# Cross attention with a mixture of experts on one core: the last batch whole in the second half, fewer warm transposes, logits read from PSUM, new orders

## The chip, the cores and the metric

The kernel runs on one core of a Trainium2 chip. The metric is the device time of one execution in microseconds (us), the median of several runs. TensorE (PE), VectorE (DVE), ScalarE (ACT), GpSimd (POOL) and SyncE (SP) each work off their own queue in order; they wait for each other on semaphores. VectorE, ScalarE and TensorE reach PSUM, eight banks of 512 fp32 columns; GpSimd works on SBUF alone.

## The reference

x is (4, 512, 128), the context is (4, 77, 96). Cut to what matters:

```python
xn = layernorm(ctx, ln_x_g, ln_x_b)                    # 77 x 96 a batch
ln = layernorm(_layernorm(x), ln_l_g, ln_l_b)          # 512 x 128 a batch
q  = ln @ Wq.T                                         # 2 heads of 64
k, v = split(concat([xn @ Wkv.T, ln @ Wlkv.T], axis=1))   # 77 + 512 keys
attn = softmax(where(mask, (rmsnorm(q)*SCALE) @ rmsnorm(k).T, -max))
x = x + (attn @ v) @ Wo.T + bo
l2 = _layernorm(x)
gates = softmax(l2 @ Wg + bg)                          # 8 experts
top2 = top_k(gates, 2)                                 # not renormalised
out = x + sum over top2 of gate * (l2 @ We[e] + be[e])
```

All is fp32. The masked context columns get the largest negative number before the softmax.

## The kernel before

Each batch is 4 tiles of 128 tokens. The first half of the work (normalise, q, k, v) is cut into the parts of FRONT, each (batch, first tile, end tile): batch 0 in two parts of two tiles, the others whole, so FRONT part 2 is batch 1, part 3 batch 2, part 4 batch 3. The second half (scores, exponentials, values, projection, second layernorm, gate, experts) is cut into the parts of REAR; before the change these are batches 0 to 2 whole and batch 3 as two parts, 3 and 4, of two tiles.

There is no scheduler at run time. Four texts, TENSOR, VECTOR, SCALAR and GPSIMD, list the jobs of each engine in the order of its queue: name, part, and a number within the part. TENSOR also names the PSUM banks that a job writes; `free` lets the job wait until the last user of each bank has been read. `walk` issues the jobs. The third number of `warm` is a slot; its second number says how many transposes of the identity that job issues, into a bank that nobody reads.

The jobs which the prediction speaks of:

- `warm` (L923), `weights` (L930, L932) and `weights2` (L940, L942): transposes of the identity, and of the weight matrices. ScalarE's `weights` and `weights2` (L498, L503, L504) copy the latter out of PSUM.
- `stats1`, `rstd1`, `apply1`, `xT`, `lnT`: first layernorm. `q`, `qsq` (square, ScalarE), `ssq` (sum, L733, VectorE), `rq` (the power -1/2, L396, GpSimd), `qn` (L742), `qT`, `QH` and `QL`: the query, split into a rounded fp32r part and the rest. `k`, `kL`, `ssk`, `msk`, `rk` (L402) are the same for keys. Scores are three matmuls each (high x high, high x low, low x high).
- `ctx_apply` (L789) and other `ctx_` jobs: the context's part of keys and values. `mask`, `maskT`, `cbias`: the mask as a bias.
- `score p n` (n = 0 to 3 for key tiles, 4 for the context), `exp p n` (L602, L605; two instructions, one a head), `value p n`. `e01`, `e23` (L421, L430, GpSimd) and `esum1`, `esum2` (L803, L810, VectorE) sum the exponentials over key tiles; `den`, `dens`, `denT` turn that sum.
- `xbo` (L442, GpSimd): x plus bias bo, into one of two buffers; from batch 2 on it waits for the `x2` of two batches earlier. `proj`, `x2` (L822, L826, L830): the first half's result. `stats2`, `rstd2` (L448 to L451), `apply2` (L629), `l2T`, `l2L`, `gate` (L1121).
- `shifted` (L378, GpSimd) and `split` (L714, L716, VectorE): expert weights less their last row, and split in two. The two DMAs of the bias row lie between them (SyncE waits for `shifted`).
- `logits` (L850 to L860), `gexp`, `top` (L868 to L873): the largest logit, the two largest, the weights w. `low` (ScalarE, L660) scales four experts' output from PSUM by w, `high` (VectorE, L892) multiplies the other four and adds them up: number n of `high` on VectorE covers two tiles, eight instructions. `pair` and `res` (L473, L474, L482, GpSimd) add the two halves, and SyncE stores (L349).

Of the kernel before, what the change touches and what calls it, by code (L numbers as in the profile page):

```python
# [1169 lines left out]
```

## Time and profile before

| | |
|---|---|
| runs | 121.44, 122.02, 121.33 us; median 121.44 |
| the profiled execution | 120.44 us |
| its span in the profile | 118.6 us |
| PE | 105.5 us busy, 89%, 733 matmuls |
| DVE | 79.4 us, 67%, 317 instructions |
| ACT | 85.9 us, 72%, 209 |
| POOL | 92.3 us, 78%, 113 |
| granted TensorE clock, mean | 0.97 |
| chain that ended last | POOL 38%, PE 27%, DVE 18%, issue 11%, ACT 3% |

The span runs from the first to the last event of the one profiled execution. A busy share is an average over stages with different limits. Ends of matmuls are modelled, so a busy PE is not one at its peak. "Idle before" in a row is the time in which the engine stood still just before the instruction, and the arrow names what released it.

### The profile page before, as it was taken

What the parts mean: (1) busy time and instruction counts of PE and PEld (TensorE: products, weight loads), DVE (VectorE), ACT (ScalarE), POOL (GpSimd) and SP (SyncE); (2) the same over time, 40 slices, a digit from 0 to 9 for tenths busy, and PEclk for the clock granted to TensorE, in tenths of its full rate; (3) what the DMA queues carried; (4) which work ended last, traced back from release to release, by engine and by line L of the source; (5) the groups of instructions that cost most, each with busy time, mean ns of one, the idle gap of its engine ahead of it and who ended that gap; (6) DMA issues with size and microseconds to landing.
All of it is one profiled execution on the core that took longest, in us unless ns stands there. A gap on an engine that the chain in (4) does not pass through costs nothing.

```text
span 118.6 us, 2507 instructions
## 1 busy us (share of the span) xinstructions
PE 105.5 (89%) x733; PEld 74.5 (63%) x733; DVE 79.4 (67%) x317; ACT 85.9 (72%) x209; POOL 92.3 (78%) x113
## 2 busy tenths in 40 slices
...
DMA packets 6679, 3.92 MB, mean 33 GB/s; under 512 B 2314, under 2 KB 6282, under 8 KB 6667
## 3 DMA queue, kind: packets, MB, share of 16 engines
...
## 4 chain that ended last, share of the span: by engine, by line
POOL 38%; PE 27%; DVE 18%; issue 11%; ACT 3%; POOLq 1%; DVEq 0%; ACTq 0%
PE PS L923 8%; DVE part L892 6%; PE PS L1068 6%; POOL esum L421 5%; PE PS L1047 5%; POOL rq L396 4%; POOL e L430 4%; POOL xbo L442 4%; POOL rk L402 3%; POOL rstd L388 3%; PE PS L1102 2%; DVE acc L892 2%; POOL pair L473 2%; POOL rstd L450 2%; POOL We L378 2%
## 5 line engine op out<-in xcount | busy, mean ns | idle before, releaser
L602 ACT ACTIVATE probs<-PS,shift,rk 128x512 f32<-128x512 f32 (+1 forms) x40 | 25.0, 694 | 4.6 <-PE PS L1047 4.4
L660 ACT ACTIVATE scaled<-PS,w 128x128 f32<-128x128 f32 x64 | 17.4, 385 | 4.6 <-PE PS L916 3.7
L1068 PE MATMUL PS<-probs,V_sb 128*64 128x512 f32 (+1 forms) x80 | 16.1, 519 | 0.0
L914 PE MATMUL PS<-WeH,l2H 128*128 128x512 f32 x32 | 13.5, 423 | 1.8 <-ACT scaled L660 0.9
L473 POOL TENSOR_TENSOR pair<-scaled 128x512 f32<-128x512 f32 x8 | 10.3, 1286 | 4.0 <-ACT scaled L660 3.6
L916 PE MATMUL PS<-WeH,l2L 128*128 128x512 f32 x32 | 12.6, 393 | 0.0
L915 PE MATMUL PS<-WeL,l2H 128*128 128x512 f32 x32 | 12.5, 391 | 0.0
L430 POOL TENSOR_TENSOR e<-probs,probs 128x1024 f32<-128x1024 f32 (+1 forms) x5 | 9.7, 1931 | 3.0 <-ACT probs L602 3.0
L421 POOL TENSOR_TENSOR esum<-probs,probs 128x1024 f32<-128x1024 f32 (+1 forms) x5 | 10.7, 2141 | 1.1 <-ACT probs L602 1.1
L923 PE MATMUL PS<-ident 128*128 128x128 f32 x60 | 9.4, 324 | 1.5 <-POOL ident L366 1.5
L1047 PE MATMUL PS<-QH,KH 64*128 64x512 f32 (+1 forms) x40 | 9.0, 435 | 1.3 <-DVE QL L773 0.7
L923 PEld LDWEIGHTS PS<-ident 128*128 128x128 f32 x60 | 8.8, 172 | 1.5 <-POOL ident L366 1.5
L629 ACT ACTIVATE l<-x,nm,rstd 128x127 f32<-128x127 f32 x16 | 6.7, 490 | 3.7 <-POOL nm L451 3.7
L402 POOL TENSOR_TENSOR rk<-msk,half 128x8 f32<-128x8 f32 (+1 forms) x5 | 7.9, 1582 | 1.5 <-DVE msk L750 1.5
L1068 PEld LDWEIGHTS PS<-probs,V_sb 128*64 128x64 f32 x80 | 4.9, 136 | 6.3 <-issue 5.1
L892 DVE SCALAR_TENSOR_TENSOR part<-PS,w,part 128x128 f32<-128x128 f32 x32 | 8.9, 336 | 0.0
L914 PEld LDWEIGHTS PS<-WeH,l2H 128*128 128x128 f32 x32 | 6.1, 191 | 4.1 <-ACT scaled L660 1.3
L803 DVE TENSOR_TENSOR esum<-esum,e 128x1024 f32<-128x1024 f32 (+1 forms) x5 | 5.5, 1107 | 4.7 <-POOL e L430 4.7
L733 DVE TENSOR_REDUCE ssq<-qsq 128x8 f32<-128x512 f32 (+1 forms) x5 | 2.9, 579 | 8.6 <-ACT qsq L535 8.6
L396 POOL TENSOR_TENSOR rq<-msq,half 128x8 f32<-128x8 f32 (+1 forms) x5 | 7.3, 1465 | 0.4
L1047 PEld LDWEIGHTS PS<-QH,KH 64*128 64x128 f32 x40 | 4.1, 189 | 5.6 <-issue 2.8
L1047 PE MATMUL PS<-QH,KL 64*128 64x512 f32 (+1 forms) x40 | 7.6, 361 | 0.0
...
## 6 DMA issues: line engine op xcount, KB each, us to landing
out_dram<-x SPq DMA_DIRECT2D x8, 128.0 KB, 1.7
...
x_sb<-in_x_dram SPq DMA_DIRECT2D x2, 128.0 KB, 2.5
Wlkv_sb<-in_L_xattn_Wlkv_dram ACTq DMA_DIRECT2D x1, 128.0 KB, 3.0
...
```

Source lines behind the costliest of these rows:

```text
L421: pool.tensor_tensor(esum[p % 2][:, :, s], probs[p % 2][0][:, :, s], probs[p % 2][1][:, :, s], ALU.add).then_inc(e01_made, 1)
L430: pool.tensor_tensor(e23[:, :, s], probs[p % 2][2][:, :, s], probs[p % 2][3][:, :, s], ALU.add).then_inc(e23_made, 1)
L473: step(pool.tensor_tensor(pair[:], scaled[m % 2][:, :, 0:EH // 2], scaled[m % 2][:, :, EH // 2:EH], ALU.add))
L602: act.activation(probs[p % 2][n][:, h, s], ps[:, s], ACT.Exp, bias=shift[:, 0:1], scale=rk[:, b, n, h:h + 1]).then_inc(probs_made, 1)
L660: last = act.activation(scaled[m // 2 % 2][:, m % 2, e], ps[:, e], ACT.Copy, scale=w[:, m, e:e + 1])
L892: last = dve.scalar_tensor_tensor(dst, bank("high", p, 2 * n + k)[:, e * C:(e + 1) * C], w[:, m, EH + e:EH + e + 1], src, ALU.mult, ALU.add)
L914: pe.matmul(dst, lH, rH, start=True, stop=False)
L915: pe.matmul(dst, lH, rL, start=False, stop=False)
L916: return pe.matmul(dst, lL, rH, start=False, stop=True)
L923: pe.transpose(bank("warm", p, n)[:, 0:P], ident[:], ident[:])
L1047: last = pe.matmul(bank("score", p, n, h)[0:P if n < T else M, 0:(e - a) * P], k, queries[r, b % 2, a * P:e * P], start=(step == 0), stop= ...
L1068: last = pe.matmul(bank("value", p, 0)[h * D:(h + 1) * D, s], v, pr, start=(n == 0), stop=(n == KT - 1))
```

## The change

REAR takes batch 3 as one part, so the second half has four parts instead of five; its score, exponential, esum, x2, logits and other instructions of that batch are over 512 columns or four tiles each. The warm transposes go from 35 + 3 + 11 + 11 = 60, all ahead of the first q, to 14 + 1 + 4 + 4 there, 1 after v 0 and 2 ahead of the first score. The four orders and the bank numbers are written anew; k 0 now comes ahead of v 0, proj 0 and x2 0 right behind the values of batch 0, and all jobs of batch 3's score stand before its gate. In `logits` the subtraction of the largest logit reads the logits from PSUM instead of the SBUF copy, the bank is released by it, and the copy of the two largest becomes a reduction over an axis of one element. `cbias` does its first step in place in PSUM.

```diff
--- before.py
+++ after.py
@@ -20,62 +20,57 @@
 
 
 FRONT = ((0, 0, 2), (0, 2, 4), (1, 0, 4), (2, 0, 4), (3, 0, 4))
-REAR = ((0, 0, 4), (1, 0, 4), (2, 0, 4), (3, 0, 2), (3, 2, 4))
+REAR = ((0, 0, 4), (1, 0, 4), (2, 0, 4), (3, 0, 4))
 
 
 
 TENSOR = """
-    warm 0 35 7   weights 0 0 0   warm 1 3 7   weights2 0 0 1   warm 2 11 7   xT 0 0 2   warm 3 11 7   q 0 0 3
-    v 0 0 4   xT 1 0 5   k 0 0 6   ctxT 0 0 7   v 1 0 0   q 1 0 1   ssk 0 0 2   ctx_v 0 0 4   qT 0 0 5   k 1 0 7
-    ctx_k 0 0 3   maskT 0 0 0   qT 1 0 4   ssk 1 0 1   ctx_ss 0 0 2   score 0 0 05   score 0 1 61   xT 2 0 4
-    score 0 2 72   score 0 3 05   k 2 0 4   q 2 0 3   v 2 0 1   value 0 0 6   value 0 1 -   value 0 2 -
...
-    high 1 1 0   high 1 2 2   l2T 3 0 7   low 1 1 6   gate 2 0 3   low 1 2 4   low 1 3 5   high 1 3 6
-    high 2 0 0   low 2 0 1   gate 3 0 4   l2T 4 0 3   low 2 1 7   low 2 2 5   gate 4 0 2   low 2 3 6   low 3 0 3
-    low 3 1 1   high 2 1 4   high 2 2 7   high 2 3 2   high 3 0 5   high 3 1 6   low 4 0 0   low 4 1 4
-    high 4 0 3   high 4 1 1
+    warm 0 14 7   weights 0 0 0   warm 1 1 7   weights2 0 0 1   warm 2 4 7   xT 0 0 2   warm 3 4 7   q 0 0 3
+    k 0 0 4   xT 1 0 5   v 0 0 6   warm 4 1 7   ssk 0 0 7   ctxT 0 0 0   q 1 0 1   k 1 0 2   ctx_v 0 0 6
+    qT 0 0 4   ssk 1 0 5   ctx_k 0 0 0   maskT 0 0 7   v 1 0 3   qT 1 0 6   ctx_ss 0 0 5   warm 5 2 1
+    score 0 0 14   score 0 1 32   score 0 2 06   xT 2 0 5   score 0 3 14   value 0 0 7   score 0 4 23   k 2 0 5
+    v 2 0 0   q 2 0 6   value 0 1 -   value 0 2 -   value 0 3 -   value 0 4 -   ssk 2 0 1   den 0 0 4
+    proj 0 0 52   xT 3 0 3   xT 4 0 0   denT 0 0 7   qT 2 0 6   v 3 0 4   q 3 0 1   q 4 0 3   k 3 0 0
+    score 1 0 42   score 1 1 57   k 4 0 6   ssk 3 0 0   qT 3 0 2   score 1 2 41   score 1 3 05   value 1 0 7
+    value 1 1 -   score 1 4 21   score 2 0 43   score 2 1 05   value 1 2 -   value 1 3 -   value 1 4 -
...
+    proj 2 0 57   score 3 3 12   score 3 4 06   denT 2 0 3   value 3 1 -   value 3 2 -   value 3 3 -
+    value 3 4 -   l2T 1 0 1   low 0 0 2   low 0 1 0   gate 1 0 6   den 3 0 3   proj 3 0 57   denT 3 0 4
+    low 0 2 1   low 0 3 2   low 1 0 0   low 1 1 3   l2T 2 0 6   high 0 2 1   high 0 3 4   high 1 0 5   high 1 1 7
+    gate 2 0 2   high 1 2 6   high 1 3 0   low 1 2 1   low 1 3 4   low 2 0 3   l2T 3 0 2   low 2 1 1   low 2 2 5
+    gate 3 0 7   low 2 3 2   low 3 0 4   low 3 1 3   low 3 2 0   high 2 0 6   high 2 1 1   high 2 2 7
+    high 2 3 5   high 3 0 2   high 3 1 4   high 3 2 1   high 3 3 6   low 3 3 3
...
 VECTOR = """
-    x2 1 0   stats2 1 0   esum1 3 0   x2 2 0   top 0 0   esum2 3 0   stats2 2 0   high 0 0   esum1 4 0
-    esum2 4 0   x2 3 0   logits 1 0   stats2 3 0   top 1 0   x2 4 0   stats2 4 0   high 0 1   high 1 0
-    logits 2 0   high 1 1   top 2 0   logits 3 0   logits 4 0   top 3 0   high 2 0   top 4 0   high 2 1
-    high 3 0   high 4 0
...
+    consts 0 0   stats1 0 0   stats1 1 0   ctx_stats 0 0   gain 0 0   ctx_apply 0 0   ssq 0 0   kL 0 0
+    shift 0 0   msk 0 0   mask 0 0   qn 0 0   ssq 1 0   stats1 2 0   msk 1 0   qn 1 0   QL 0 0   kL 1 0
+    ctx_kL 0 0   QL 1 0   ctx_ms 0 0   stats1 3 0   stats1 4 0   cbias 0 0   kL 2 0   ssq 2 0   esum1 0 0
+    esum2 0 0   split 0 0   qn 2 0   msk 2 0   x2 0 0   QL 2 0   ssq 3 0   stats2 0 0   kL 3 0   qn 3 0   ssq 4 0
+    msk 3 0   QL 3 0   qn 4 0   kL 4 0   esum1 1 0   esum2 1 0   msk 4 0   logits 0 0   QL 4 0   top 0 0
+    high 0 0   esum1 2 0   x2 1 0   esum2 2 0   stats2 1 0   x2 2 0   stats2 2 0   esum1 3 0   esum2 3 0
+    logits 1 0   x2 3 0   stats2 3 0   top 1 0   high 0 1   logits 2 0   high 1 0   top 2 0   high 1 1
+    logits 3 0   top 3 0   high 2 0   high 2 1   high 3 0   high 3 1
...
 SCALAR = """
...
-    l2T 0 0   v 4 0   exp 3 0   dens 2 0   exp 3 1   oT 2 0   exp 3 2   exp 3 3   exp 3 4   exp 4 0   gexp 0 0
-    exp 4 1   exp 4 2   apply2 1 0   oT 3 0   exp 4 3   exp 4 4   l2T 1 0   dens 3 0   apply2 2 0   low 0 0
-    low 0 1   oT 4 0   dens 4 0   gexp 1 0   low 0 2   low 0 3   low 1 0   apply2 3 0   l2T 2 0   low 1 1
...
+    lnT 4 0   QH 2 0   v 3 0   qsq 3 0   qsq 4 0   k 3 0   exp 1 0   exp 1 1   QH 3 0   exp 1 2   exp 1 3
+    apply2 0 0   exp 1 4   k 4 0   exp 2 0   oT 1 0   l2T 0 0   exp 2 1   v 4 0   exp 2 2   QH 4 0   gexp 0 0
+    exp 2 3   dens 1 0   exp 2 4   exp 3 0   oT 2 0   exp 3 1   exp 3 2   dens 2 0   exp 3 3   exp 3 4
+    apply2 1 0   oT 3 0   l2T 1 0   low 0 0   low 0 1   dens 3 0   apply2 2 0   low 0 2   low 0 3   gexp 1 0
...
 GPSIMD = """
-    ident 0 0   blanks 0 0   rstd1 0 0   rstd1 1 0   ctx_rstd 0 0   rq 0 0   rq 1 0   rstd1 2 0   rk 0 0
-    xbo 0 0   rk 1 0   xbo 1 0   rstd1 3 0   ctx_rk 0 0   e01 0 0   rq 2 0   e23 0 0   rstd1 4 0   shifted 0 0
-    rk 2 0   rq 3 0   rk 3 0   e01 1 0   rq 4 0   e23 1 0   xbo 2 0   e01 2 0   rstd2 0 0   e23 2 0   rk 4 0
-    l2L 0 0   e01 3 0   e23 3 0   xbo 3 0   xbo 4 0   rstd2 1 0   e01 4 0   e23 4 0   rstd2 2 0   l2L 1 0
-    pair 0 0   rstd2 3 0   res 0 0   pair 0 1   rstd2 4 0   res 0 1   l2L 2 0   pair 1 0   l2L 3 0   res 1 0
-    pair 1 1   l2L 4 0   res 1 1   pair 2 0   pair 2 1   res 2 0   pair 3 0   res 2 1   pair 4 0   res 3 0
-    res 4 0
+    ident 0 0   blanks 0 0   rstd1 0 0   rstd1 1 0   ctx_rstd 0 0   rq 0 0   rk 0 0   rq 1 0   rstd1 2 0   rk 1 0
+    ctx_rk 0 0   rstd1 3 0   rstd1 4 0   e01 0 0   e23 0 0   shifted 0 0   rq 2 0   xbo 0 0   xbo 1 0   rk 2 0
+    xbo 2 0   rq 3 0   rstd2 0 0   rq 4 0   e01 1 0   rk 3 0   e23 1 0   l2L 0 0   rk 4 0   e01 2 0   e23 2 0
+    xbo 3 0   e01 3 0   rstd2 1 0   e23 3 0   rstd2 2 0   l2L 1 0   pair 0 0   res 0 0   pair 0 1   rstd2 3 0
+    res 0 1   l2L 2 0   pair 1 0   res 1 0   l2L 3 0   pair 1 1   res 1 1   pair 2 0   pair 2 1   res 2 0
+    pair 3 0   res 2 1   pair 3 1   res 3 0   res 3 1
...
@@ -295,7 +289,7 @@
             "denT": lambda p, n: (x2_made, p + 1),
             "proj": lambda p, n: (x2_made, p + 1),
             "l2T": lambda p, n: (l2T_made, p + 1),
-            "gate": lambda p, n: (lg_made, p + 1),
+            "gate": lambda p, n: (lgs_made, p + 1),
             "low": lambda p, n: (scaled_made, tile_number(p, n) + 1),
             "high": lambda p, n: (acc_made, tile_number(p, n) + 1),
         }
@@ -703,10 +697,10 @@
             def cbias_(p, n):
 
                 dve.wait_ge(maskT_done, 1)
-                dve.wait_ge(dve_step, step(dve.tensor_scalar(mbias[:], bank("maskT", 0, 0)[0:M, 0:B], 1.0, MASKED,
-                                                             ALU.subtract, ALU.mult)))
+                seen = bank("maskT", 0, 0)[0:M, 0:B]
+                dve.wait_ge(dve_step, step(dve.tensor_scalar(seen, seen, 1.0, MASKED, ALU.subtract, ALU.mult)))
                 dve.wait_ge(shift_made, 1)
-                dve.tensor_scalar(cbias[:], mbias[:], shift[0:M, 0:1], None, ALU.add).then_inc(cbias_made, 1)
+                dve.tensor_scalar(cbias[:], seen, shift[0:M, 0:1], None, ALU.add).then_inc(cbias_made, 1)
 
             def split_(p, n):
 
@@ -847,15 +841,13 @@
                 g, s = e - a, slice(b * T + a, b * T + e)
                 dve.wait_ge(gate_done, p + 1)
                 dve.wait_ge(pads_made, 1)
-                dve.tensor_copy(lg[:, s, 0:E], bank("gate", p, 0)[:, 0:g * E].rearrange("p (t e) -> p t e",
-                                                                                       e=E)).then_inc(lg_made, 1)
-                dve.wait_ge(lg_made, p + 1)
+                logits = bank("gate", p, 0)[:, 0:g * E].rearrange("p (t e) -> p t e", e=E)
+                dve.wait_ge(dve_step, step(dve.tensor_copy(lg[:, s, 0:E], logits)))
                 for t in range(b * T + a, b * T + e):
                     last = dve.max(top[:, t], lg[:, t, 0:E])
                 dve.wait_ge(dve_step, step(last))
-                dve.tensor_tensor(lgs[:, s], lg[:, s, 0:E], top[:, s, 0:1].to_broadcast([P, g, E]),
-                                  ALU.subtract).then_inc(lgs_made, 1)
-                dve.wait_ge(dve_step, step(dve.tensor_copy(two[:, s, 0:2], top[:, s, 0:2])))
+                dve.tensor_tensor(lgs[:, s], logits, top[:, s, 0:1].to_broadcast([P, g, E]), ALU.subtract).then_inc(lgs_made, 1)
+                dve.wait_ge(dve_step, step(dve.tensor_reduce(two[:, s, 0:2], top[:, s, 0:2].unsqueeze(3), AX.X, ALU.max)))
                 for t in range(b * T + a, b * T + e):
                     last = dve.match_replace(marked[:, t, 0:E + 6], two[:, t], lg[:, t, 0:E + 6], CHOSEN)
                 step(last)
```

## Rows read from the trace of the kernel before

**Rows 1.** Table of stretches: from:to, length, busy us of each engine, clock, DMA.

```profile
19.70:23.10 3.40, 3.40 (x16) 2.28 (x14) 2.01 (x15) 2.55 (x6) 3.39 (x4) 0.51 0.00 0
23.10:42.00 18.90, 18.90 (x129) 11.83 (x128) 8.03 (x12) 17.24 (x33) 18.13 (x17) 1.00 0.01 2
42.00:62.00 20.00, 19.29 (x135) 10.71 (x134) 9.73 (x27) 16.45 (x28) 18.30 (x13) 1.00 0.01 1
62.00:80.00 18.00, 17.05 (x168) 11.40 (x167) 15.01 (x65) 14.58 (x34) 12.26 (x12) 1.00 0.01 2
91.40:103.00 11.60, 10.59 (x55) 8.11 (x53) 11.36 (x52) 7.17 (x25) 11.14 (x16) 1.00 0.11 35
111.30:118.60 7.30, 0.04 (x1) 0.00 (x0) 4.34 (x17) 0.40 (x2) 4.47 (x6) 0.77 0.16 54
```

**Rows 2.** Instructions in order of time, 1 to 13 us: start, length, engine, line.

```profile
1.15 0.46 ACTq L490 DMA_DIRECT2D Wlkv_sb<-in_L_xattn_Wlkv_dram  x1
1.51 6.20 PE L923 MATMUL PS<-ident 128*128 128x128 f32 x35 [1.51 <-POOL ident L366]
8.07 0.48 ACT L498 COPY WT<-PS 128x384 f32<-128x384 f32 x1 [4.11 <-PE PS L932]
8.44 1.04 DVE L789 TENSOR_SCALAR cxh<-ctx_sb,cmv,crstd 77x96 f32<-77x96 f32 x4 [1.08 <-POOL crstd L408]
12.21 0.42 DVE L733 TENSOR_REDUCE ssq<-qsq 128x4 f32<-128x256 f32 x1 [2.73 <-ACT qsq L535]
```

**Rows 3.** DMA issues of the page: size, median us from issue to landing.

```profile
Wlkv_sb<-in_L_xattn_Wlkv_dram ACTq DMA_DIRECT2D x1, 128.0 KB, 3.0
```

**Rows 4.** Order of time, 36 to 53 us, and line L442's durations.

```profile
36.13 2.37 POOL L378 TENSOR_TENSOR We<-We_sb,We_end 128x1024 f32<-128x1024 f32 x1
40.45 0.69 DVE L714 CAST WeH<-We 128x1024 fp32r<-128x1024 f32 x1 [1.40 <-DMA Wg<-in_L_ffn_bg_dram]
42.69 0.69 DVE L742 TENSOR_TENSOR qn<-PS,rq 128x512 f32<-128x512 f32 x1 [0.29 <-POOL rq L396]
52.24 2.12 POOL L442 TENSOR_TENSOR xbo<-x_sb,bo_b 128x512 f32<-128x512 f32 x1 [1.20 <-DVE x L830]
...
L442 POOL TENSOR_TENSOR xbo<-x_sb,bo_b x5: 730/1271/2120, 19.4 to 72.9; 128x512 f32<-128x512 f32 x3, 128x256 f32<-128x256 f32 x2
```

**Rows 5.** Order of time, ScalarE's exponentials, 51 to 75 us.

```profile
51.24 4.78 ACT L602 ACTIVATE probs<-PS,shift,rk 128x512 f32<-128x512 f32 x7
66.10 1.02 ACT L602 ACTIVATE probs<-PS,shift,rk 128x256 f32<-128x256 f32 x2 [2.07 <-PE PS L1047]
72.72 2.13 ACT L602 ACTIVATE probs<-PS,shift,rk 128x256 f32<-128x256 f32 x4
```

**Rows 6.** Groups by shape, VectorE: busy us, mean ns, idle before.

```profile
L803 DVE TENSOR_TENSOR esum<-esum,e 128x1024 f32<-128x1024 f32 x3 | 3.7, 1222 | 4.7 <-POOL e L430 4.7
L810 DVE TENSOR_TENSOR esum<-esum,probs 77x512 f32<-77x512 f32 x2 | 2.5, 1240 | 0.0
L803 DVE TENSOR_TENSOR esum<-esum,e 128x512 f32<-128x512 f32 x2 | 1.9, 936 | 0.0
```

**Rows 7.** Lines L856 and L858 (min/median/max ns), and order of time at 85.8 us.

```profile
L856 DVE TENSOR_TENSOR lgs<-lg,top x5: 178/281/1309, 65.7 to 103.5; 128x32 f32<-128x32 f32 x3, 128x16 f32<-128x16 f32 x2
L858 DVE COPY two<-top x5: 156/165/1309, 65.8 to 103.6; 128x8 f32<-128x8 f32 x3, 128x4 f32<-128x4 f32 x2
...
85.79 1.28 POOL L473 TENSOR_TENSOR pair<-scaled 128x512 f32<-128x512 f32 x1 [2.57 <-ACT scaled L660]
85.80 1.31 DVE L856 TENSOR_TENSOR lgs<-lg,top 128x32 f32<-128x32 f32 x1
```

**Rows 8.** Order of time, first and last step of batch 0's chain after stats2.

```profile
57.70 0.24 POOL L448 TENSOR_SCALAR nmean<-mv 128x4 f32<-128x4 f32 x1
64.00 1.06 PE L1121 MATMUL PS<-Wg,l2T 128*128 128x8 f32 x8
```

**Rows 9.** Order of time, VectorE's last `high`: its first two and last two instructions.

```profile
113.51 0.59 DVE L892 SCALAR_TENSOR_TENSOR part<-PS,w,x 128x128 f32<-128x128 f32 x2
115.06 0.59 DVE L892 SCALAR_TENSOR_TENSOR acc<-PS,w,part 128x128 f32<-128x128 f32 x2
```

More of the change, by code:

```diff
@@ new lines @@
+    proj 0 0 52   xT 3 0 3   xT 4 0 0   denT 0 0 7   qT 2 0 6   v 3 0 4   q 3 0 1   q 4 0 3   k 3 0 0
+    score 1 0 42   score 1 1 57   k 4 0 6   ssk 3 0 0   qT 3 0 2   score 1 2 41   score 1 3 05   value 1 0 7
+    value 1 1 -   score 1 4 21   score 2 0 43   score 2 1 05   value 1 2 -   value 1 3 -   value 1 4 -
+    score 2 2 12   l2T 0 0 6   ssk 4 0 3   qT 4 0 4   v 4 0 7   gate 0 0 6   high 0 0 3   high 0 1 0
+    proj 1 0 57   score 2 3 12   den 1 0 6   value 2 0 4   value 2 1 -   value 2 2 -   score 2 4 12
@@ new lines @@
+    score 3 0 60   denT 1 0 3   value 2 3 -   value 2 4 -   score 3 1 12   score 3 2 06   value 3 0 4   den 2 0 3
+    proj 2 0 57   score 3 3 12   score 3 4 06   denT 2 0 3   value 3 1 -   value 3 2 -   value 3 3 -
+    value 3 4 -   l2T 1 0 1   low 0 0 2   low 0 1 0   gate 1 0 6   den 3 0 3   proj 3 0 57   denT 3 0 4
+    low 0 2 1   low 0 3 2   low 1 0 0   low 1 1 3   l2T 2 0 6   high 0 2 1   high 0 3 4   high 1 0 5   high 1 1 7
+    gate 2 0 2   high 1 2 6   high 1 3 0   low 1 2 1   low 1 3 4   low 2 0 3   l2T 3 0 2   low 2 1 1   low 2 2 5
@@ L52 @@
-    esum2 0 0   msk 2 0   kL 3 0   msk 3 0   QL 2 0   ssq 3 0   split 0 0   qn 3 0   ssq 4 0   QL 3 0   qn 4 0
-    x2 0 0   esum1 1 0   stats2 0 0   esum2 1 0   kL 4 0   esum1 2 0   msk 4 0   esum2 2 0   QL 4 0   logits 0 0
-    x2 1 0   stats2 1 0   esum1 3 0   x2 2 0   top 0 0   esum2 3 0   stats2 2 0   high 0 0   esum1 4 0
-    esum2 4 0   x2 3 0   logits 1 0   stats2 3 0   top 1 0   x2 4 0   stats2 4 0   high 0 1   high 1 0
-    logits 2 0   high 1 1   top 2 0   logits 3 0   logits 4 0   top 3 0   high 2 0   top 4 0   high 2 1
@@ L67 @@
-    low 0 1   oT 4 0   dens 4 0   gexp 1 0   low 0 2   low 0 3   low 1 0   apply2 3 0   l2T 2 0   low 1 1
-    apply2 4 0   low 1 2   l2T 3 0   gexp 2 0   low 1 3   l2T 4 0   low 2 0   low 2 1   gexp 3 0   low 2 2
-    low 2 3   gexp 4 0   low 3 0   low 3 1   low 4 0   low 4 1
+    weights 0 0   apply1 0 0   weights2 0 0   lnT 0 0   apply1 1 0   qsq 0 0   k 0 0   v 0 0   lnT 1 0   ctxT 0 0
+    qsq 1 0   k 1 0   ctx_v 0 0   QH 0 0   ctx_k 0 0   v 1 0   QH 1 0   apply1 2 0   exp 0 0   exp 0 1   lnT 2 0
```

27 lines of the change are left out of this document (5 added, 22 removed).

## The prediction

> **What bounds the kernel now.** I read the busy line of the page first, then the table of stretches, the order of time at the start, the landings, the order of time again where batches follow each other, and last the groups by shape. No engine is full all along (the table of the profile has their shares), so the stretches count. From 23.1 to 62 us GpSimd is at work 18.13 of 18.9 and 18.30 of 20.0 us. From 62 to 80 VectorE has 15.0 and ScalarE 14.6 of 18. From 91.4 to 103 VectorE has 11.36 of 11.6, and after 111.3 TensorE does nothing while VectorE and GpSimd finish [rows 1]. So the start of GpSimd's row of jobs sets the middle, ScalarE with its releases of PSUM the part after it, and VectorE the end. TensorE's column overstates it, since ends of matmuls are modelled, but it leaves little room in the second half.
>
> The start holds the surprise. The 35 warm transposes run from 1.51 to 7.71 us, and the weight transposes stand behind them in TensorE's queue. But the last attention weight that these need was issued at 1.15 us and took 3.0 us to land: 4.15. ScalarE idled 4.11 us until the WT copy at 8.07, and its queue holds apply1 behind that copy [rows 2, 3]. So some 3.5 us of the start are spent behind transposes that nobody reads.
>
> The profiled execution took 120.44 us, 1.84 more than its span of 118.6; the median of the runs is 121.44, 1.00 above it. I sum against the profiled one and add the 1.00.
>
> **Warm transposes: 60 become 26.** The 35 took 0.177 us each on the mean [rows 2]. At that pace the new 14 end at 4.0, and at 0.22, if only the later ones were quick, at 4.6. Behind them come three weight transposes (0.6 at most), so the WT copy starts near 5.3 instead of 8.07. From that copy to ssq 0 at 12.21 the trace has 4.14 us [rows 2], which would put ssq 0 at 9.4, and earlier still as 22 more warm transposes on that way become 8. But VectorE's queue has ctx_apply ahead of ssq 0; it waits for a power from GpSimd, not for TensorE, and ran to 9.48 [rows 2]. So ssq 0 starts at 9.5: 2.7 us gained. I take 0.5 off for the clock. One stretch, 19.70 to 23.10, ran at a granted 0.51, the 1.2 GHz level, after TensorE had had short gaps, and the new start has fewer matmuls to fill gaps. Such a stretch of 3.4 us costs at most 1.7 us of matmul work [rows 1], most of it beside waits for VectorE and GpSimd. Front: 2.2 us. Bounds: 2.7, and -1.0 if two such stretches lie wholly on the path (3.4) and 0.3 is lost on the weights.
>
> The Trainium skill (TensorE: Matmul & The Clock Gate, What's actually happening) says that the array runs at half rate unless recent activity has released it. That speaks against cutting warm transposes, and by it the front could come to nothing, which is the rival on the clock below. The trace agrees so far as its own low stretch goes [rows 1].
>
> **New orders, the middle.** GpSimd does the same jobs, so what it gains is its earlier start, the front's 2.2. Two of its moves count. rk 0 and rk 1 come ahead of the xbo jobs (1.27 us each in the median [rows 4]), so the first exponentials start sooner, but no job is saved. And xbo 2, rstd2 0 and l2L 0 come early; xbo 2 needs x2 0. Where is that? `shifted` ended at 38.50 [rows 4]. The front (2.2), xbo 0 and 1 (2.5) and rq 2 (2.0, half of the two jobs below) go from ahead of it, so it ends at 31.8. SyncE then issues the two bias DMAs, which kept VectorE's split waiting until 40.45 [rows 4], 1.95 later: 33.75. Split takes 0.69 and a 1024-column pass of 1.22 [rows 4, 6], to 35.7; qn 2 and msk 2 about 0.9, x2 0 eight instructions of the kind of `high` (2.1 for eight [rows 9]) and two reciprocals, 2.5: 39.1. GpSimd after `shifted` has rq 2, rk 2, xbo 0 and xbo 1. One rk and one rq filled 38.66 to 42.66, when qn 3 was released [rows 4]: 4.0, with 2.5 for xbo, so it stands at xbo 2 at 38.3 and waits 0.8 us, where the wait was 1.20 before [rows 4]. Behind it stand rq 3, rstd2 0, rq 4, e01 1 and rk 3, and for those wait qn 3, the scores of batch 2 and apply2 0. No net change there: 0, between -1 and 1.
>
> **Last batch whole.** Twenty exponentials of 256 columns become ten of 512. Four of the short ones in a row took 2.13 us (0.533 each), seven of the long 4.78 (0.683 each) [rows 5]: 10.66 - 6.83 = 3.8 us off ScalarE. The 2.07 us in which it waited for the first scores of batch 3 [rows 5], behind QL 4, goes too, as rq 4 now stands well ahead of e23 2. That is 5.9 us between 62 and 80, where ScalarE with 14.58 of 18 us and VectorE with 15.01 take turns in holding the rest up [rows 1]. TensorE has the same columns to do, and was shown busy 17.05 of 18 there [rows 1]. I take a third, 2.0 us, as what comes out; bounds 0 (TensorE truly full) and 5.9.
>
> VectorE: a half pass of esum2 took 1.24 and of esum1 0.94, two of each; a whole esum1 took 1.22, and esum2, the same operation on as many columns, is taken as that [rows 6]: 2.48 + 1.88 - 2.44 = 1.9 us less. One set of logits, top and reciprocals less, about eight instructions of 0.16 to 0.2: 1.3 us. GpSimd loses one rstd2 (about 0.8 us net).
>
> What it costs: the last chain (x2, stats2, rstd2, apply2, l2T, gate, logits, gexp, top) is for four tiles instead of two. In the new VECTOR order the stats of batch 3 are followed by top 1, three `high`, logits 2, top 2, logits 3, top 3 and four `high`. A `high` is eight instructions in 2.1 us (the last from 113.5 to 115.65) [rows 9], so top 1, three `high`, logits 2 and top 2 are some 9 us of cover. Batch 0's chain took 7.4 us from rstd2's first step (57.70) to the end of its gate matmuls (65.06) [rows 8]. It is hidden.
>
> **Logits from PSUM, the reduce for the copy.** The copy of top took 0.165 in the median and once 1.309, the subtraction 0.281 and once 1.309. That subtraction began 0.01 us after a GpSimd `pair` of 1.28 us and ended with it [rows 7]. Without these waits the two save 1.15 and 1.1 = 2.3 us; bounds 0, if the next two-input instruction (ew, w) takes the wait over, and 2.3. The `gate` bank is freed by the subtraction rather than the copy, 0.6 us later, but TensorE comes back to that bank only many jobs later (after gate 0 with score 3 0), so this is priced at 0. The mask's in-place step removes nothing measurable (0.15 us, before the first score): 0, within 0.1 either way.
>
> The Trainium skill (SBUF — State Buffer, Who interferes with whom) has a rule for it: VectorE and GpSimd share a port pair under an exclusive lock, taken by VectorE instructions with two SBUF inputs and by fast copies, not by one with a single SBUF input, nor by a reduce. By it both edits are free of the wait, the upper bound; a wait moved on to ew, which keeps two SBUF inputs, would be the lower.
>
> **Tail sum.** 1.9 + 1.3 + 2.3 = 5.5 us off VectorE after 62 us. TensorE leaves little of it to gain until 103, but after it stops VectorE and GpSimd run on for 4.3 and 4.5 us of work [rows 1], which is VectorE's lag; a lag that shrinks by about one `high` is worth 2.1, less 0.6 because TensorE now ends with a `low` whose ScalarE and GpSimd steps follow: 1.5. Bounds -1.0 (that last low on the path whole, no lag gained) and 5.5.
>
> Sum: 2.2 + 2.0 + 1.5 = 5.7; 118.6 - 5.7 = 112.9 us of span, 114.7 profiled, 115.7 median.
>
> **The rivals.** TensorE full (27 in 100): its matmuls in the second half are the bound, and only the front and 0.6 us of the tail show: 118.6 us. For it, 17.05 of 18 us in 62 to 80 [rows 1]. Against it, ScalarE sat idle 2.07 us there until a score came, and the score itself had waited: a full engine makes others wait without waiting [rows 5].
>
> The clock (5): the start stays at the low level until the first scores, the front gives nothing, 117.9 us. For it, the stretch at 19.7 [rows 1]; against, that only 3.4 us were low there.
>
> Nothing (8): GpSimd's later jobs and the coarser last batch give back what the front gains, 121.2 us.
>
> Slower (12): GpSimd's in-order queue at xbo 2. If x2 0 is made not at 39.1 but later, each us delays rq 3 and all behind it, the scores of batches 2 and 3 with them. The point is 5.7 us: beyond 44.8 the change loses. xbo 2 was released at 52.24 before [rows 4], so this is no remote place; at 47 it has lost 7.9 us against the 39.1, of which the 5.7 gained take off all but 2.2, and the time is 123.6 us. For it: x2 0 hangs on the bias DMA, split, den, proj in one chain; against: its 39.1 is bound by split, while den and proj of batch 0 need only esum and oT and have time beside it.
>
> **How the numbers follow.** The forecast has 48 in 100, with 113.2 to 117.8 for itself. Half a per cent, 0.6 us, is what a measurement can tell here. Faster: 48 + 27 + 5 = 80; same 8; slower 12. The range runs from 112.0 (all bounds of front and tail near the upper end) to 120.8, leaving out the same and slower cases.
>
> **What would show it.** WT copy at about 5.3, ssq 0 at 9.5, x2 0 before 41, all exponentials over by 74, lgs and two never above 0.4 us, last matmul near 106.5. The forecast is wrong if ssq 0 is later than 11, if GpSimd stands idle over 4 us ahead of xbo 2, or if TensorE has no gap from 60 on and still ends after 109.

## The result

The changed kernel takes 113.94 us (median of four runs, 113.84 to 115.13) against 121.56 for the kernel before in the same comparison (121.33 to 122.02): ratio 0.939, 95% interval 0.932 to 0.946, 7.6 us less. The forecast was 115.7, with 112.0 to 120.8 as its range. The profiled execution took 113.98 us, with a span of 112.2 and a mean granted clock of 0.962. Where runs of one kernel lay over 1.5% above its fastest, the medians and differences in this document leave them out, while the ranges in brackets are of all runs.

The order of time at the start of the changed kernel, on TensorE, ScalarE and VectorE (start, length; compare [rows 2]):

```profile
1.51 3.25 PE L915 MATMUL PS<-ident 128*128 128x128 f32 x14 [1.51 <-POOL ident L360]
...
5.13 0.48 ACT L492 COPY WT<-PS 128x384 f32<-128x384 f32 x1 [1.17 <-PE PS L924]
...
9.68 0.41 DVE L727 TENSOR_REDUCE ssq<-qsq 128x4 f32<-128x256 f32 x1
...
17.39 0.76 ACT L596 ACTIVATE probs<-PS,shift,rk 128x512 f32<-128x512 f32 x1
```

The copy of WT comes 2.9 us earlier, ssq 0 2.5 us, the first exponential at 17.39 instead of 20.06. The idle time ahead of the copy fell from 4.11 to 1.17 us.

The middle of the changed kernel, rows taken from the orders of time of GpSimd (POOL), VectorE (DVE), TensorE (PE) and ScalarE (ACT) (compare [rows 4]):

```profile
26.64 2.38 POOL L372 TENSOR_TENSOR We<-We_sb,We_end 128x1024 f32<-128x1024 f32 x1
28.96 1.20 POOL L373 TENSOR_TENSOR Wg<-Wg_sb,Wg_end 128x8 f32<-128x8 f32 x1
...
26.80 3.30 DVE L797 TENSOR_TENSOR esum<-esum,e 128x1024 f32<-128x1024 f32 x1 [0.85 <-POOL e L424]
...
31.90 0.69 DVE L708 CAST WeH<-We 128x1024 fp32r<-128x1024 f32 x1 [0.55 <-DMA Wg<-in_L_ffn_bg_dram]
...
36.08 0.25 DVE L816 RECIPROCAL rden<-PS 128x4 f32<-128x4 f32 x2 [1.55 <-PE PS L1082]
...
37.60 1.13 DVE L824 SCALAR_TENSOR_TENSOR x<-PS,rden,x2a 128x128 f32<-128x128 f32 x4
...
31.45 0.65 PE L1073 MATMUL PS<-esum,ones 128*32 128x256 f32 x8 [2.29 <-issue]
...
38.90 1.29 POOL L436 TENSOR_TENSOR xbo<-x_sb,bo_b 128x512 f32<-128x512 f32 x1 [1.04 <-DVE x L824]
...
35.20 1.45 ACT L521 ACTIVATE lnT<-PS,ln_cols 128x512 f32<-128x512 f32 x2 [2.67 <-PE PS L947]
...
40.96 2.79 ACT L596 ACTIVATE probs<-PS,shift,rk 128x512 f32<-128x512 f32 x4
```

x2 0 ends at 38.73; before it was what released xbo 2 at 52.24 [rows 4]. But batch 1's first exponential comes at 40.96, no earlier than before (40.40). In the middle the lead of 2.7 us was exchanged for a batch 0 that is 13 us ahead. One can see where: esum1 of batch 0 took 3.30 us beside GpSimd's subtraction (1.22 alone [rows 6]). TensorE stood still for 2.29 us ahead of den 0, which needs the sum that esum1 and esum2 make; the profile names no releaser for it, and esum2 ended at 31.35, 0.10 us before it. ScalarE's lnT 3, whose transposes stood behind den 0, waited 2.67 us.

The table of stretches of the changed kernel (from:to, length, busy us of PE, PEld, DVE, ACT, POOL, clock, DMA; compare [rows 1]):

```profile
19.70:23.10 3.40, 3.40 (x19) 1.49 (x18) 0.00 (x0) 3.40 (x6) 3.10 (x7) 1.00 0.00 0
...
28.00:31.00 3.00, 1.17 (x10) 0.97 (x8) 2.97 (x2) 2.60 (x7) 2.92 (x3) 1.00 0.00 0
...
31.00:35.00 4.00, 3.54 (x29) 2.93 (x30) 2.95 (x5) 0.37 (x1) 3.92 (x4) 0.62 0.02 5
...
62.00:80.00 18.00, 17.88 (x124) 8.90 (x120) 13.22 (x48) 14.00 (x28) 13.02 (x11) 1.00 0.00 1
...
91.40:103.00 11.60, 11.30 (x53) 8.64 (x53) 10.33 (x47) 9.72 (x36) 10.94 (x13) 1.00 0.07 25
103.00:110.00 7.00, 2.06 (x9) 1.31 (x7) 5.84 (x23) 2.13 (x8) 6.50 (x8) 0.79 0.11 37
```

The stretch with the low level of the clock (1.2 GHz) did not grow: 3.4 us at a mean of 0.51 before, 4.0 us at a mean of 0.62 now. It moved from 19.7 to 31 us, behind the 2.3 us in which TensorE waited for den 0. From 62 us on TensorE has hardly a gap. Its last matmul ends at 105.1, 7.1 us ahead of the span's end; before it was 7.3 (111.3 of 118.6 [rows 1]).

The last step of each batch's routing is the product `w`, behind which VectorE's `high` steps stand. VectorE's four `w` in the changed kernel, and the end of its last `high`:

```profile
60.33 0.19 DVE L865 TENSOR_TENSOR w<-ew,erc 128x32 f32<-128x32 f32 x1
...
86.51 0.70 DVE L865 TENSOR_TENSOR w<-ew,erc 128x32 f32<-128x32 f32 x1
...
93.64 0.70 DVE L865 TENSOR_TENSOR w<-ew,erc 128x32 f32<-128x32 f32 x1
...
99.84 0.69 DVE L865 TENSOR_TENSOR w<-ew,erc 128x32 f32<-128x32 f32 x1
...
108.25 0.60 DVE L884 SCALAR_TENSOR_TENSOR acc<-PS,w,part 128x128 f32<-128x128 f32 x2
```

In the kernel before, the first `w` came at 77.30 and the last at 108.84. So batch 0's comes 17.0 us earlier and the last one 9.0. Behind the last `w` stand four `high` of 2.1 us, without a gap, and 3.4 us of GpSimd and store. That is the end of the program: it is set by when the last `w` comes and by how many `high` are still due.

### The profile page after: what moved, and what is told of

It reads as the page before. It is cut to its first block and busy times, and to the rows that moved or that the text cites. A ratio compares the mean times of both kernels' runs of the same rounds, so it can differ in the third digit from the quotient of the medians.

```text
span 112.2 us, 2248 instructions
## 1 busy us (share of the span) xinstructions
PE 99.7 (89%) x641; PEld 67.5 (60%) x641; DVE 76.7 (68%) x306; ACT 84.0 (75%) x194; POOL 91.2 (81%) x105
## 5 line engine op out<-in xcount | busy, mean ns | idle before, releaser
L596 ACT ACTIVATE probs<-PS,shift,rk 128x512 f32<-128x512 f32 x32 | 22.6, 780 | 3.1 <-PE PS L1039 3.1
L1060 PE MATMUL PS<-probs,V_sb 128*64 128x512 f32 x64 | 15.5, 605 | 0.0
L424 POOL TENSOR_TENSOR e<-probs,probs 128x1024 f32<-128x1024 f32 x4 | 9.5, 2371 | 1.5 <-ACT probs L596 1.5
L436 POOL TENSOR_TENSOR xbo<-x_sb,bo_b 128x512 f32<-128x512 f32 x4 | 6.5, 1632 | 5.2 <-DVE x L824 5.2
L415 POOL TENSOR_TENSOR esum<-probs,probs 128x1024 f32<-128x1024 f32 x4 | 9.5, 2377 | 0.0
L797 DVE TENSOR_TENSOR esum<-esum,e 128x1024 f32<-128x1024 f32 x4 | 6.9, 1736 | 2.6 <-POOL e L424 2.6
L599 ACT ACTIVATE probs<-PS,cbias,crk 77x512 f32<-77x512 f32 x8 | 5.7, 769 | 2.4 <-PE PS L1039 2.4
L1039 PE MATMUL PS<-QH,KH 64*128 64x512 f32 x32 | 7.2, 439 | 0.4 <-DVE QL L767 0.4
L507 ACT ACTIVATE xh<-x_sb,nm,rstd 128x128 f32<-128x128 f32 x16 | 6.7, 490 | 0.6 <-POOL nm L383 0.6
L908 PEld LDWEIGHTS PS<-WeH,l2L 128*128 128x128 f32 x32 | 6.0, 188 | 1.5
```

The lines of the kernel that those rows point to most:

```text
L415: pool.tensor_tensor(esum[p % 2][:, :, s], probs[p % 2][0][:, :, s], probs[p % 2][1][:, :, s], ALU.add).then_inc(e01_made, 1)
L424: pool.tensor_tensor(e23[:, :, s], probs[p % 2][2][:, :, s], probs[p % 2][3][:, :, s], ALU.add).then_inc(e23_made, 1)
L596: act.activation(probs[p % 2][n][:, h, s], ps[:, s], ACT.Exp, bias=shift[:, 0:1], scale=rk[:, b, n, h:h + 1]).then_inc(probs_made, 1)
L908: return pe.matmul(dst, lL, rH, start=False, stop=True)
L1039: last = pe.matmul(bank("score", p, n, h)[0:P if n < T else M, 0:(e - a) * P], k, queries[r, b % 2, a * P:e * P], start=(step == 0), stop= ...
L1060: last = pe.matmul(bank("value", p, 0)[h * D:(h + 1) * D, s], v, pr, start=(n == 0), stop=(n == KT - 1))
```

## The experiments

A comparison has its own runs of the kernel before, whose medians were 121.40, 121.20 and 121.80 us in the three of this section. A term below is good to about 1 us unless an interval is given.

**The parts alone, in the old orders.** Theory: each term of the sum is worth about what was forecast (2.2 the front, 2.0 the whole batch, 1.5 the tail). Rival: the parts only pay together with the new orders.

b_warm: the kernel before with the four warm counts of the changed kernel.

```diff
-    warm 0 35 7  ...  warm 1 3 7  ...  warm 2 11 7  ...  warm 3 11 7
+    warm 0 14 7  ...  warm 1 1 7  ...  warm 2 4 7  ...  warm 3 4 7
```

> The kernel before, only its four warm jobs changed to 14, 1, 4 and 4 transposes. Front theory (the start waits behind unread transposes, and GpSimd's row of jobs carries an earlier start to the end): 2.2 us faster than before, ssq 0 at 9.5 us instead of 12.21, batch 1's first exponential at 38.2 instead of 40.40. Rival (the start is slack, the middle is set by something else, and only the new orders can use it): within 0.6 us of before, though ssq 0 is early. Rival on the clock: the start stays at the 1.2 GHz level and ssq 0 comes after 11 us.

118.63 us (118.50 to 118.93), ratio 0.978 (0.973 to 0.983): 2.8 us less. The copy of WT was at 5.44, the first exponential at 17.08 and that of batch 1 at 37.4, 3.0 earlier. The front is real, at the forecast's 2.2 or up to 1 us above it.

b_whole: batch 3 as one part in the old orders; jobs of part 4 are dropped or renamed to part 3.

```diff
-REAR = ((0, 0, 4), (1, 0, 4), (2, 0, 4), (3, 0, 2), (3, 2, 4))
+REAR = ((0, 0, 4), (1, 0, 4), (2, 0, 4), (3, 0, 4))
-    l2L 0 0   e01 3 0   e23 3 0   xbo 3 0   xbo 4 0   rstd2 1 0   e01 4 0   e23 4 0   rstd2 2 0
+    l2L 0 0   e01 3 0   e23 3 0   xbo 3 0   rstd2 1 0   rstd2 2 0
```

> The kernel before with batch 3 whole in the second half, in the old orders (the jobs of part 4 are struck out or become numbers of part 3). Sum theory: ScalarE is 3.8 us lighter and VectorE 3.2 us, and 2.0 to 3.5 us of it come out. Rival (the coarser last batch needs the new orders, since its chain stands late in the old ones): within 1 us of before or slower. Rival (TensorE full from 60 us on): within 0.6 us.

122.84 us (122.84 to 126.08): 1.4 us slower, on one run, so how much slower is open; none of its runs was faster than the kernel before. The exponentials did end 4.5 us earlier (75.2 instead of 79.7), as the term had it. What came then is in its order of time, GpSimd and then ScalarE:

```profile
73.92 2.36 POOL L426 TENSOR_TENSOR e<-probs,probs 128x1024 f32<-128x1024 f32 x1 [0.80 <-ACT probs L598]
76.24 1.27 POOL L438 TENSOR_TENSOR xbo<-x_sb,bo_b 128x512 f32<-128x512 f32 x1
77.48 1.20 POOL L444 TENSOR_SCALAR nmean<-mv 128x4 f32<-128x4 f32 x1
...
80.37 1.65 ACT L625 ACTIVATE l<-x,nm,rstd 128x127 f32<-128x127 f32 x4 [5.08 <-POOL nm L447]
```

ScalarE gave its gain back standing idle for 5.1 us: its next job, apply2 1, needs rstd2 1, and on GpSimd rstd2 1 stands behind e23 3 and xbo 3. The last `w` came at 108.16 instead of 108.84, but four `high` stand behind it instead of three. In the new orders rstd2 1 stands ahead of e23 3, and ScalarE starts the same job at 74.80, the moment the exponentials end.

b_psum: the three edits of the code alone.

```diff
-                dve.tensor_tensor(lgs[:, s], lg[:, s, 0:E], top[:, s, 0:1].to_broadcast([P, g, E]),
+                dve.tensor_tensor(lgs[:, s], logits, top[:, s, 0:1].to_broadcast([P, g, E]),
-                dve.wait_ge(dve_step, step(dve.tensor_copy(two[:, s, 0:2], top[:, s, 0:2])))
+                dve.wait_ge(dve_step, step(dve.tensor_reduce(two[:, s, 0:2], top[:, s, 0:2].unsqueeze(3), AX.X, ALU.max)))
```

> The kernel before with the three edits of code alone: the subtraction reads the logits from PSUM, the copy of the two largest is a reduction, the mask's first step is in place in PSUM. Sum theory: VectorE 2.3 us lighter, half of it comes out, 0.5 to 1.5 us faster; lgs and two never above 0.3 us. Rival (the waits move to the next instructions with two SBUF inputs, ew and w): within 0.5 us, and ew and w longer on the mean than 0.53 and 0.48 us.

117.32 us (117.29 to 119.86): 4.1 us less, on two runs. VectorE's lgs, two, ew and w together went from 9.4 to 6.7 us, and ew and w were as long as before on the mean (0.55 and 0.45), so no wait moved on to them. Not all of the gain can be put down to them: its profiled execution already had batch 1's first exponential at 39.74 instead of 40.40 and batch 2's at 49.88 instead of 50.56, ahead of any logits. Where the rest comes from is open.

b_all: all three together, still in the old orders.

> The kernel before with the warm counts, the whole batch and the code edits, but in the old orders. If the parts of my sum are right and the orders are worth nothing: 5 to 6 us faster, as the changed kernel. If the new orders carry the gain: 1 to 3.5 us faster, and the rest of the 7.6 us belongs to the orders.

118.48 us (118.43 to 121.50), ratio 0.976 (0.968 to 0.984): 2.9 us less, on two runs. That is what the front alone gives, and not the sum of the three (-2.8 + 1.4 - 4.1 = -5.5): in the old orders the parts do not add up. The changed kernel differs from this one by the orders, the bank numbers and 3 warm transposes placed behind q 0. So the new orders carry about 4.5 of the 7.6 us (3 to 6, by the intervals), and they were priced at 0.

**The parts taken out of the changed kernel.**

a_warm60: the old 60 warm transposes in the new orders.

> The changed kernel with the 60 warm transposes of before (35, 3, 11, 11) in place of 26. Theory: a front that ends about 3 us later moves the whole program, in the new orders as it did in the old ones (there 3.0 us): 116.5 to 117. Rival: in the new orders part of the front's gain is spent in the wait of TensorE for den 0 and of ScalarE for lnT 3 (2.3 and 2.7 us), so the later front costs only 0 to 1.5 us: 114.0 to 115.5.

115.80 us (115.55 to 118.64), ratio 0.957 (0.947 to 0.967): 1.9 us worse, on two runs, between the two expectations. Its last `w` came at 101.8 instead of 99.8. So the front is worth about 2 us in the new orders, less than the 2.8 in the old ones, and the run does not say whether the rest is spent in the wait for den 0.

a_nopsum: the three code edits undone.

> The changed kernel with the three edits of the code undone (mask bias through its own tile, lgs read from the copy in SBUF after a semaphore, two by tensor_copy). Theory: their 2.2 us in the old orders came from long waits of lgs and two behind GpSimd's pair; in the new orders VectorE is 90% busy in the last stage and the same waits return: 115.8 to 116.2. Rival: the new orders have moved these instructions away from pair, so they cost 0 to 0.6: 114.0 to 114.6.

114.07 us (112.75 to 115.23), ratio 0.940 (0.932 to 0.949): the same as the changed kernel. The rival was right. The groups of VectorE's instructions by shape (busy us, mean ns), first of this kernel:

```profile
L865 DVE SCALAR_TENSOR_TENSOR ew<-marked,eg 128x32 f32<-128x32 f32 x4 | 2.5, 631 | 0.0
...
L868 DVE TENSOR_TENSOR w<-ew,erc 128x32 f32<-128x32 f32 x4 | 2.3, 568 | 0.1
...
L851 DVE TENSOR_TENSOR lgs<-lg,top 128x32 f32<-128x32 f32 x4 | 1.5, 366 | 0.1
...
L853 DVE COPY two<-top 128x8 f32<-128x8 f32 x4 | 0.6, 162 | 0.0
```

and of the changed kernel:

```profile
L862 DVE SCALAR_TENSOR_TENSOR ew<-marked,eg 128x32 f32<-128x32 f32 x4 | 2.7, 672 | 0.0
...
L865 DVE TENSOR_TENSOR w<-ew,erc 128x32 f32<-128x32 f32 x4 | 2.3, 571 | 0.1
...
L849 DVE TENSOR_TENSOR lgs<-PS,top 128x32 f32<-128x32 f32 x4 | 0.8, 191 | 0.1
...
L850 DVE TENSOR_REDUCE two<-top 128x8 f32<-128x8 f32 x4 | 0.6, 152 | 0.0
```

6.9 against 6.4 us: the edits save 0.5 us of VectorE here, since `two` no longer meets a `pair` in these orders. The waits that are left sit in ew and w, whose inputs are both in SBUF and which the change leaves alone (the shortest `w` took 0.19 us).

**Which part of the orders.** Theory: batch 0's chain, brought forward, takes work out of the last stage. Rival: it fills idle time, and the gain is in the order of the last 20 us.

a_late0: the whole output chain of batch 0 late again, in all four orders; shown are two moves on TensorE.

```diff
-    proj 0 0 52   xT 3 0 3   xT 4 0 0   denT 0 0 7   ...
+    xT 3 0 3   xT 4 0 0   ...
...
-    value 1 1 -   score 1 4 21   score 2 0 43   ...
+    value 1 1 -   score 1 4 21   denT 0 0 6   proj 0 0 52   score 2 0 43   ...
...
```

> The changed kernel with the output chain of batch 0 late as before: proj 0, denT 0 and x2 0 after the scores of batch 1, the transposes, gate, logits of batch 0 between batch 2's scores, its two first high products after the values of batch 3. Theory A: the chain brought forward is what carries most of the 6 us of the new orders, because it takes two high products and the router of batch 0 out of the last stage, in which VectorE and TensorE are full: 117 to 119. Theory B: it only fills idle time and the gain lies in the order of the last 20 us: 114 to 115.5.

135.09 us (134.90 to 137.49): 21 us worse, outside both expectations, so it decides nothing between them. TensorE's two longest waits after 42 us make up 10.2 of it (in order of time):

```profile
50.46 0.44 PE L1081 MATMUL PS<-ident,den_sb 128*128 128x128 f32 x2 [3.29 <-DVE KL L752]
...
81.51 0.79 PE L1038 MATMUL PS<-QH,KH 64*128 64x512 f32 x2 [6.91 <-DVE lgs L848]
```

TensorE stood for PSUM banks that were released only behind other jobs of VectorE's queue: batch 3's first scores wait 6.9 us for the bank of gate 0. Where the rest of the 21 us lies is open.

a_high0: one thing moved, the first two `high` products of batch 0 and their eight steps on VectorE.

```diff
-    score 2 2 12   l2T 0 0 6   ssk 4 0 3   qT 4 0 4   v 4 0 7   gate 0 0 6   high 0 0 3   high 0 1 0
+    score 2 2 12   l2T 0 0 6   ssk 4 0 3   qT 4 0 4   v 4 0 7   gate 0 0 6
-    ...   low 1 1 3   l2T 2 0 6   ...
+    ...   low 1 1 3   high 0 0 5   high 0 1 7   l2T 2 0 6   ...
-    ...   top 0 0   high 0 0   esum1 2 0   ...   top 1 0   high 0 1   ...
+    ...   top 0 0   esum1 2 0   ...   top 1 0   high 0 0   high 0 1   ...
```

> The changed kernel with one thing moved: the first two high products of batch 0 (TensorE 2.4 us) and VectorE's eight accumulations on them (2.7 us) go from the middle of the program, where VectorE is half idle, back behind the products low 1 1, into the last stage. Theory A: what the new orders gain is work of the last stage done earlier, and VectorE is at 90% there: 116 to 117. Theory B: there is slack elsewhere in the last stage: 114.0 to 114.8.

116.74 us (116.53 to 117.83), ratio 0.961 (0.956 to 0.967): 2.8 us worse, the size that theory A gave. Up to batch 3's exponentials it ran like the changed kernel (batch 1 from 40.9, batch 2 from 54.7). Then its last `w` and last `high` step came 2.7 us later. The rows, of GpSimd, ScalarE and VectorE:

```profile
87.57 0.75 POOL L475 TENSOR_TENSOR x<-low,acc 128x256 f32<-128x256 f32 x1 [4.24 <-DVE acc L883]
...
92.26 1.64 ACT L622 ACTIVATE l<-x,nm,rstd 128x127 f32<-128x127 f32 x4 [1.93 <-POOL nm L444]
...
102.57 0.69 DVE L864 TENSOR_TENSOR w<-ew,erc 128x32 f32<-128x32 f32 x1
...
110.98 0.60 DVE L883 SCALAR_TENSOR_TENSOR acc<-PS,w,part 128x128 f32<-128x128 f32 x2
```

The size fits theory A, but its reason is not what the trace shows. VectorE did not run out of room: from 91.4 to 103 it was busy 8.81 of 11.6 us, in the changed kernel 10.33. What the move made late is in GpSimd's queue: `res 0 0` waits for the first `high`, and stood still for 4.24 us, while rstd2 3, which the router of batch 3 needs, stands two jobs behind it. So apply2 3 on ScalarE started at 92.26 instead of 89.44, 2.8 us later, and the last `w` 2.7 us later. The move also took the two products to a later place on TensorE, whose last matmul ended at 107.8 instead of 105.1. No run separates GpSimd's wait, VectorE's eight steps and TensorE's two products: a kernel with the steps and products late and rstd2 3 ahead of `res 0 0` would.

a_split and a_split2: batch 3 in halves again in the new orders. In the first the second half's scores come behind the first's values; in the second, whose edit on TensorE is shown in part, they are woven in, and the gate of batch 1 and two low products stand among them.

```diff
-REAR = ((0, 0, 4), (1, 0, 4), (2, 0, 4), (3, 0, 4))
+REAR = ((0, 0, 4), (1, 0, 4), (2, 0, 4), (3, 0, 2), (3, 2, 4))
...
-    score 3 4 06   denT 2 0 3   value 3 1 -  ...  value 3 4 -   l2T 1 0 1   low 0 0 2
+    score 3 4 06   score 4 0 12   denT 2 0 3   value 3 0 4   value 3 1 -   score 4 1 06  ...
```

> The changed kernel with its last batch in two halves again, the second half's scores after the first's values, everything else in the new orders. Theory A (batch 3 whole is worth something once the orders fit it): ScalarE's exponentials take 3.8 us longer and end near 78.5 instead of 74.9: 116 to 118. Theory B (as in the old orders, where halves were 3.9 us faster): 112 to 113.5.

> The changed kernel with batch 3 in two halves again, this time woven in: the second half's scores between the first half's values, gate and l2T of batch 1 among them, den 4 behind low products. Theory A (whole is worth something once the orders fit it, since ScalarE then has 3.8 us less, VectorE 5.5 less): 116 to 119. Theory B (the first half's output chain beside the second half's exponentials is worth more than that, as in the old orders, where halves were 3.9 us faster): 110 to 113.

130.14 (129.00 to 132.14) and 128.55 us (128.40 to 131.71), 16 and 15 us worse. Until 62 us they keep within about 1 us of the changed kernel (batch 0's `w` at 61.34 in a_split2). Then, in a_split2, on VectorE and TensorE in turn:

```profile
84.59 0.19 DVE L846 COPY lg<-PS 128x32 f32<-128x32 f32 x1 [5.68 <-PE PS L1114]
...
90.39 0.65 PE L1074 MATMUL PS<-esum,ones 128*32 128x128 f32 x8 [3.90 <-issue]
```

From 80 to 91.4 us TensorE was busy 7.5 of 11.4 us there, against 11.4 in the changed kernel. Waits like these are much more than the price of the halves themselves, which the prediction puts at 3.8 us of exponentials at most, so both runs say little about it. What halves would cost in orders made for them is open.

**The wait for den 0.** Theory: the wait is on the path. Rival: the first exponential of batch 1 is held by the rest of the chain. a_xT puts the eight transposes that ScalarE waited for ahead of den 0.

```diff
-    ...   ssk 2 0 1   den 0 0 4   proj 0 0 52   xT 3 0 3   xT 4 0 0   denT 0 0 7   ...
+    ...   ssk 2 0 1   xT 3 0 3   xT 4 0 0   den 0 0 4   proj 0 0 52   denT 0 0 7   ...
```

> The changed kernel with the transposes xT 3 and xT 4 issued ahead of den 0 on TensorE, which waits 2.3 us for esum there while ScalarE waits 2.7 us for just these transposes. Theory A (this wait is on the path): 111.5 to 113. Theory B (batch 1's first exponential is set by the rest of the chain of q, qn, QL 2, which GpSimd's rq 2 delays): 113.5 to 114.3.

112.98 us (112.57 to 113.29), ratio 0.928 (0.923 to 0.932), the fastest version here; its interval and the changed kernel's meet at the edge, and between the medians lies 1.0 us. Its order of time, TensorE and then ScalarE:

```profile
29.30 0.64 PE L947 MATMUL PS<-ident,xh 128*128 128x128 f32 x4
31.02 0.89 PE L947 MATMUL PS<-ident,xh 128*128 128x128 f32 x4 [1.08 <-ACT xh L507]
31.84 1.08 PE L1073 MATMUL PS<-esum,ones 128*32 128x256 f32 x8
...
40.21 2.79 ACT L596 ACTIVATE probs<-PS,shift,rk 128x512 f32<-128x512 f32 x4
```

TensorE no longer stands ahead of den 0, but 1.08 us ahead of the second group of transposes, and ScalarE no longer ahead of lnT 3, but 2.1 us ahead of den's copy. Batch 1's first exponential moved by 0.75 us, not by 2.3: theory A with the smallest gain that it allowed. QL 2, which its scores need, stands behind x2 0 on VectorE and came at 37.90 instead of 38.64. a_xTrq also puts rq 2 ahead of the subtraction on GpSimd.

```diff
-    ...   e23 0 0   shifted 0 0   rq 2 0   ...
+    ...   e23 0 0   rq 2 0   shifted 0 0   ...
```

> The same as before it, and rq 2 ahead of the subtraction of the bias from We (2.4 us on GpSimd). Theory A (both waits are on the path to batch 1's first exponential): 110.5 to 112.5. Theory B (VectorE's esum and x2 0 ahead of QL 2 hold it anyway): 113.3 to 114.3.

116.96 us (116.56 to 118.02), ratio 0.962 (0.956 to 0.968): 4.0 worse than a_xT, against both theories. Its order of time, VectorE, GpSimd, ScalarE:

```profile
26.82 1.25 DVE L797 TENSOR_TENSOR esum<-esum,e 128x1024 f32<-128x1024 f32 x1 [0.57 <-POOL e L424]
...
33.84 1.28 DVE L708 CAST WeH<-We 128x1024 fp32r<-128x1024 f32 x1 [4.52 <-DMA Wg<-in_L_ffn_bg_dram]
...
27.14 2.44 POOL L390 TENSOR_TENSOR rq<-msq,half 128x8 f32<-128x8 f32 x1
29.56 2.35 POOL L372 TENSOR_TENSOR We<-We_sb,We_end 128x1024 f32<-128x1024 f32 x1
...
43.93 2.79 ACT L596 ACTIVATE probs<-PS,shift,rk 128x512 f32<-128x512 f32 x4
```

I had left a queue out. VectorE's split stands ahead of qn 2, and it waits for the two bias DMAs, which SyncE issues only behind the subtractions of `shifted`. With rq 2 ahead of them the first DMA was issued at 32.09 instead of 30.19; VectorE stood 4.5 us for it, split's first step took 1.28 instead of 0.69, and qn 2, for whose sake rq 2 was moved, came at 36.29 instead of 33.59. The stall of 2 us that the move took from esum1 (1.25 instead of 3.30) bought nothing.

## Why the prediction was right, and where it was not

The time came out 1.8 us below the forecast of 115.7, within the range, but the terms did not add up as written. The three parts that were to bring 5.7 us bring 2.9 without the orders (b_all), and the orders, priced at 0, bring about 4.5. That the two errors, 2.8 us too much and about 4.5 too little, leave only 1.8 is luck.

- *The front, 2.2.* Right: 2.8 alone in the old orders, about 1.9 in the new. WT at 5.13 (5.3), ssq 0 at 9.68 (9.5). The 0.5 us taken off for the clock was not lost at the start: 19.7 to 23.1 ran at 1.00, and the low stretch came at 31, behind a wait of TensorE for den 0.
- *New orders, the middle, 0.* This is the step that failed. x2 0 ended at 38.73 (39.1) and xbo 2 waited 1.04 (0.8), but not by the chain that was forecast. Split ran from 31.90 to 33.86, 1.8 us ahead of the forecast, and x2 0 then waited 1.55 us for the transposes of den 0. The prediction had x2 0 "bound by split", with time to spare for den and proj; it was the other way round, and the close hit is luck. The slower rival's point of 44.8 was never near. The step asked only whether xbo 2 would block the queue. It did not ask what an x2 0 that is 13 us early is good for: `w` of batch 0 comes 17 us early, and the first `high` of VectorE, with its two products on TensorE, leaves the last stage. To put these back costs 2.8 us (a_high0), by the trace through GpSimd's queue. Rstd2 1 ahead of e23 3 keeps ScalarE from 5 us of idle time (read by comparing b_whole with the changed kernel, not tried alone). How the 4.5 us divide is open.
- *Last batch whole, 2.0.* By itself it brought nothing in the old orders (122.84 us, 1.4 slower), although all exponentials were over 4.5 us earlier. "I take a third, 2.0 us, as what comes out" had no row behind it. What decides is whether ScalarE's next job is ready, and that was to be read in GpSimd's order, where rstd2 1 stood behind e23 3 and xbo 3. In the changed kernel the exponentials were over at 74.9 (forecast: by 74).
- *Logits from PSUM, in the tail's 5.5.* lgs never above 0.20 us and two never above 0.16, as said. The edits went with 4.1 us in the old orders, of which 2.7 us of VectorE's time are seen, and with 0.1 in the new. The sum added them to orders that had already parted these instructions from `pair`.
- *Tail, 1.5.* The mechanism failed. VectorE's busy time fell by 2.7 us (79.4 to 76.7), not by 5.5: the four esum1 took 1.74 us each on the mean, against 1.22 alone, and ew 0.67. VectorE's last step ended 4.3 us behind TensorE's last matmul before and 3.8 after, the program 7.3 and 7.1. The tail came earlier as a whole because the last `w` did.
- *TensorE full.* The rival's time, 118.6, is out. From 42 us to its last matmul TensorE was busy 65.7 of 69.3 us before and 62.6 of 63.1 in the changed kernel, so 3.2 us of its gaps are gone. By this column, whose ends are modelled, it has almost no gap left there, and that it bounds the changed kernel is not ruled out by any run. Last matmul at 105.1 (106.5 forecast).

On the port, the Trainium skill (SBUF — State Buffer, Who interferes with whom) calls the pair of ports that VectorE and GpSimd share an exclusive lock, and says that issue order decides who blocks. The traces agree: esum1, begun 0.16 us behind GpSimd's subtraction, took 3.30 us, about its own 1.22 and the 2.2 left of the other; and GpSimd's Wg of eight elements, begun at 28.96, took 1.20 us (0.20 in a_xTrq, where VectorE stood idle) and ended just after esum1.
